# Attention's output: row sums fetched with the products and divided on VectorE

## The reference

```python
w = jax.nn.softmax(scores, axis=-1)
attn = jnp.einsum('bhqk,bkhd->bqhd', w, v).reshape(Bb, Tt, D_MODEL)
return attn @ W_o
...
x = x + ga * _L0_attn_ref(h, ...)
```

## Time and profile before

| | us |
|---|---|
| median of 3 runs | 2197.97 |
| the three runs | 2193.12, 2197.97, 2199.91 |
| the profiled execution | 2178.26 |
| its span in the profile | 2176.7 |

### The profile page before, as it was taken

One profiled execution on the slowest core, in us unless ns is written; L12 is line 12 of the kernel. 1 busy time (PEld: TensorE's weight loads), 2 busy tenths in 40 slices (PEclk: granted clock), 3 DMA queues, 4 the chain that ended last, 5 costly groups with the idle time before them and its releaser, 6 DMA issues. The chain is left out here.

```text
span 2176.7 us, 34681 instructions
## 1 busy us (share of the span) xinstructions
PE 1704.2 (78%) x12628; PEld 841.7 (39%) x12628; DVE 1213.1 (56%) x3101; ACT 859.0 (39%) x1137; POOL 288.6 (13%) x356
## 2 busy tenths in 40 slices
PE   4775268999999999899999366304888887999888
PEld 3332012333333333333333142202444454998566
DVE  3576587877886978687870035301545545101466
ACT  0232034565665666566667204202555513000143
POOL 1000384000000000000000030273222100000011
PEclk8898589999999999999999686656999968999989
DMA  5233942130303030303010130026666200773011
GB/s 174 101 119 136 177 136 71 39 61 26 74 24 65 25 74 26 75 25 74 14 37 26 60 130 0 27 107 152 154 158 153 78 5 6 261 234 121 1 39 48
DMA packets 88965, 180.41 MB, mean 83 GB/s; under 512 B 12529, under 2 KB 61330, under 8 KB 83538
## 3 DMA queue, kind: packets, MB, share of 16 engines
q1 hardware_dynamic: 69072, 109.73, 20.0%
q0 software_dynamic: 18656, 66.31, 9.0%
q10 hardware_dynamic: 1090, 2.36, 0.3%
HBM read 119.38 MB, written 57.85 MB: 81 GB/s over the span
## 5 line engine op out<-in xcount | busy, mean ns | idle before, releaser
L858 ACT ACTIVATE at_pr<-ps 128x1024 f32<-128x1024 f32 (+3 forms) x640 | 548.8, 894 | 358.5 <-PE ps L798 230.3
L892 DVE TENSOR_REDUCE at_mx<-ps 128x1 f32<-128x512 f32 x768 | 488.8, 685 | 168.1 <-PE ps L748 158.5
L795 PE MATMUL ps<-at_sq,at_sk 64*128 64x512 f16 (+3 forms) x2560 | 344.1, 347 | 21.6 <-DMA at_sq<-at_mr 17.8
L748 PE MATMUL ps<-at_sk,at_sq 64*128 64x512 f16 (+3 forms) x1280 | 235.9, 365 | 112.6 <-DMA at_vl<-d_va 41.2
L774 PE MATMUL ps<-at_pr,at_vl 128*32 128x512 f32 (+3 forms) x2560 | 300.6, 541 | 0.1
L889 DVE CUSTOM_DVE_ANT_0 at_seen<-ps,later 128x384 bf16<-128x384 f32 (+3 forms) x512 | 230.0, 488 | 5.4 <-issue 3.8
L798 PE MATMUL ps<-bq,bk 64*128 64x512 f16 (+3 forms) x1280 | 223.9, 346 | 0.0
L748 PEld LDWEIGHTS ps<-at_sk,at_sq 64*128 64x128 f16 x1280 | 61.9, 93 | 409.0 <-DVE at_mx L892 219.1
L795 PEld LDWEIGHTS ps<-at_sq,at_sk 64*128 64x128 f16 x2560 | 112.1, 95 | 126.8 <-ACT at_pr L858 35.7
L1698 PE MATMUL ps<-mi_vn,mi_tz 128*128 x1024 | 144.0, 303 | 2.3 <-DMA mi_tz<-d_z 2.3
L1698 PEld LDWEIGHTS ps<-mi_vn,mi_tz 128*128 128x128 f32 x1024 | 141.4, 191 | 5.1 <-issue 2.7
(11 more groups left out here) (239 smaller groups left out, 2086.8 us busy)
## 6 DMA issues: line engine op xcount, KB each, us to landing
mi_tz<-d_z SPq DMA_DIRECT2D x32, 1024.0 KB, 5.1
ex_w<-d_w POOLq DMA_DIRECT2D x23, 768.0 KB, 6.9
d_rows<-at_nil POOLq DMA_DIRECT2D x32, 379.5 KB, 2.9
ex_xr<-d_rows SPq DMA_DIRECT2D x23, 512.0 KB, 8.2
d_va<-pj_va SPq DMA_DIRECT2D x8, 1024.0 KB, 3.9
at_vl<-d_va SPq DMA_DIRECT2D x8, 1024.0 KB, 12.8
d_o<-at_oc POOLq DMA_DIRECT2D x32, 256.0 KB, 2.3
at_pw<-in_w POOLq DMA_DIRECT2D x24, 256.0 KB, 3.2
```

The costliest lines, as they stand in the source:

```text
L748: ins = pe.matmul(ps[:, MAXB + (slot + r) % RING, 0:hi_ - lo], sq[half[r], b, i, 0, qb * P:(qb + 1) * P], sk[half[r], b, i, 0, lo:hi_], st ...
L795: pe.matmul(ps[:, 2 * f + r, off:CH], sk[half[r], b, f, part, k], sq[half[r], b, f, part, q], start=part == 0, stop=False)
L858: act.activation(pr[:, n % 2, f, :, off:CH], ps[:, 2 * f:2 * f + 2, off:CH], ACT.Exp, scale=INV_SCALE).then_inc(exp_done[f], 1)
L892: ins = dve.tensor_reduce(dst, src, AX.X, ALU.max)
```

## The change

The table of reciprocals in DRAM goes, and with it the loads of `sums`, their two reciprocals, the stores and the loads of `rb`. The chunk loop has three buffers in place of two. For each chunk SP loads the products as before, and ACT's DMA queue loads `total`, rows 16 to 31 of each head, which are 16 equal rows of sums: the same shape as the products. VectorE takes the reciprocal of all of `total` in place (128x1024), and multiplies products and reciprocals into `on`, in place of POOL. It does this for chunk n+1 before it adds the two halves of chunk n to x. TensorE's part is unchanged.

```diff
--- before.py
+++ after.py
@@ -950,50 +950,34 @@
 
         ps = g.ps
         N = NB * NCH
-        sums = sb("sums", [P, NB, T // 8])
-        inv = sb("inv", [P, NB, T // 8])
-        ou = sb("ou", [P, 2, KT, CH])
-        rb = sb("rb", [P, 2, KT, CH])
+        BUF = 3
+        ou = sb("ou", [P, BUF, KT, CH])
+        total = sb("total", [P, BUF, KT, CH])
         on = sb("on", [P, 2, KT, CH])
-        sums_ld = [sem(f"sums_ld{b}") for b in range(NB)]
+        o_ld = [sem(f"o_ld{x}") for x in range(BUF)]
+        t_ld = [sem(f"t_ld{x}") for x in range(BUF)]
         inv_ready = sem("inv_ready")
-        inv_st = [sem(f"inv_st{b}") for b in range(NB)]
-        o_ld = [sem(f"o_ld{x}") for x in range(2)]
         on_ready, w_ready, x_done = sem("on_ready"), sem("w_ready"), sem("x_done")
         d_heads = g.d_o.rearrange("g (h r) n -> (g h) r n", r=32)
         block = c.enter_context(nc.Block())
 
         @block.sync
         def _(sp):
-            for b in range(NB):
-                for h in range(NH):
-                    sp.dma_start(sums[8 * h:8 * h + 8, b, :],
-                                 d_heads[h, HD, b * T:(b + 1) * T].rearrange("(c n) -> c n", c=8))\
-                      .then_inc(sums_ld[b], 16)
-            for b in range(NB):
-                sp.wait_ge(inv_ready, b + 1)
-                sp.dma_start(g.d_r[b].rearrange("h (c n) -> (h c) n", c=8), inv[:, b, :]).then_inc(inv_st[b], 16)
             for n in range(N):
-                b, cols = n // NCH, slice((n % NCH) * CH, (n % NCH + 1) * CH)
-                if n >= 2:
-                    sp.wait_ge(on_ready, n - 1)
+                if n >= BUF:
+                    sp.wait_ge(on_ready, n - BUF + 1)
                 for k in range(KT):
-                    sp.dma_start(ou[:, n % 2, k, :], d_heads[8 * k:8 * k + 8, 0:HD, n * CH:(n + 1) * CH])\
-                      .then_inc(o_ld[n % 2], 16)
-                if n % NCH == 0:
-                    sp.wait_ge(inv_st[b], 16)
+                    sp.dma_start(ou[:, n % BUF, k, :], d_heads[8 * k:8 * k + 8, 0:HD, n * CH:(n + 1) * CH])\
+                      .then_inc(o_ld[n % BUF], 16)
+
+        @block.scalar
+        def _(act):
+            for n in range(N):
+                if n >= BUF:
+                    act.wait_ge(on_ready, n - BUF + 1)
                 for k in range(KT):
-                    sp.dma_start(rb[:, n % 2, k, :],
-                                 g.d_r[b, 8 * k:8 * k + 8, cols].unsqueeze(1).to_broadcast([8, HD, CH]))\
-                      .then_inc(o_ld[n % 2], 16)
-
-        @block.gpsimd
-        def _(pool):
-            for n in range(N):
-                pool.wait_ge(o_ld[n % 2], 16 * 2 * KT * (n // 2 + 1))
-                if n >= 2:
-                    pool.wait_ge(w_ready, 2 * (n - 1))
-                pool.tensor_tensor(on[:, n % 2], ou[:, n % 2], rb[:, n % 2], ALU.mult).then_inc(on_ready, 1)
+                    act.dma_start(total[:, n % BUF, k, :], d_heads[8 * k:8 * k + 8, HD:32, n * CH:(n + 1) * CH])\
+                       .then_inc(t_ld[n % BUF], 16)
 
         @block.tensor
         def _(pe):
@@ -1013,14 +997,24 @@
 
         @block.vector
         def _(dve):
-            for b in range(NB):
-                dve.wait_ge(sums_ld[b], 16 * NH)
-                dve.reciprocal(inv[:, b, :], sums[:, b, :]).then_inc(inv_ready, 1)
-            for m in range(2 * N):
-                dve.wait_ge(w_ready, m + 1)
-                xs = g.x[:, 2 * m:2 * m + 2, :]
-                dve.tensor_tensor(xs, xs, ps[:, m % 8, :].rearrange("p (t c) -> p t c", t=2), ALU.add)\
-                   .then_inc(x_done, 1)
+            def divide(n):
+                dve.wait_ge(t_ld[n % BUF], 16 * KT * (n // BUF + 1))
+                dve.reciprocal(total[:, n % BUF], total[:, n % BUF]).then_inc(inv_ready, 1)
+                dve.wait_ge(o_ld[n % BUF], 16 * KT * (n // BUF + 1))
+                if n >= 2:
+                    dve.wait_ge(w_ready, 2 * (n - 1))
+                dve.wait_ge(inv_ready, n + 1)
+                dve.tensor_tensor(on[:, n % 2], ou[:, n % BUF], total[:, n % BUF], ALU.mult).then_inc(on_ready, 1)
+
+            divide(0)
+            for n in range(N):
+                if n + 1 < N:
+                    divide(n + 1)
+                for m in (2 * n, 2 * n + 1):
+                    dve.wait_ge(w_ready, m + 1)
+                    xs = g.x[:, 2 * m:2 * m + 2, :]
+                    dve.tensor_tensor(xs, xs, ps[:, m % 8, :].rearrange("p (t c) -> p t c", t=2), ALU.add)\
+                       .then_inc(x_done, 1)
 
 
 def phase_route(nc, g):
@@ -1986,7 +1980,6 @@
         g.d_krh = dram("d_krh", [DR, NB * T], F16)
         g.d_va = dram("d_va", [P, NB * NT, NH * 32], F32)
         g.d_o = dram("d_o", [NG, P, NB * T], F32)
-        g.d_r = dram("d_r", [NB, NH, T], F32)
         g.d_w = dram("d_w", [E, P, 3 * 2 * KT * C], F16)
         g.d_rows = dram("d_rows", [NCK * CH, ROW], I32)
         g.d_ws = dram("d_ws", [2, CH], I32)
```

## The result

The changed kernel takes 2206.41 us (median of 17 runs, 2199.16 to 2216.93) against 2194.68 us (17 runs, 2185.05 to 2202.96) for the kernel before. The ratio is 1.0056, with a 95% interval of 1.0040 to 1.0072: slower by 11.7 us, or 9 to 16 us by the interval. The forecast was 13 us slower, 2211 in a range of 2203 to 2220.

A forecast was written before the change was run, and what follows sets the result against it. Loads set the old steps; VectorE would take over the pace. Start 1234.3, eight divisions 62.6, six add pairs 8.3 and tail 6.6 end at 1311.8 against 1298.05: 13 us more after overlap, 2211, range 2203 to 2220.

The forecast's parts named there:

- The bound before: Phase of 72.75 us before: head through DRAM 26.6, seven steps paced by loads at 5.36, tail 4.5; VectorE mostly idle.
- First chunk after 9 us: Head: first chunk lands 9 us after loads start at 1225.30, VectorE starts at 1234.3; bounds 7.3 and 12.0 us.
- One reciprocal 6.56 us: VectorE's 128x1024 reciprocal takes 6.56 us, from 6.25 ns per element on four lengths; bounds 1.75 and 7.01.
- cheap-reciprocal rival: Price per instruction: VectorE's reciprocal of 1024 takes 1.75 us, transfers keep the pace, 19 us less, 2179; chance 0.04.
- Product 1.23 us: VectorE's 128x1024 f32 product takes 1.23 us, priced from one with f16 output; POOL's 2.34 is the other bound.
- Division 7.83 us, cadence 9.2: VectorE per chunk: reciprocal plus product 7.83 us; with two adds of 0.69, 9.2 us against 5.36 of transfers.
- Tail 6.6 us: After the last division, matmuls and two adds take 6.6 us; 4.5 with TensorE warm, 8.5 all cold.
- Loads hidden from chunk 1 on: With three buffers a load has about 18 us and needs 8 to 12, so VectorE sets the pace.
- much slower rival: Chunk loads from two queues stay at 82 GB/s, 12.8 us per chunk; 46 us more, 2244; chance 0.03.
- The sum: Phase ends at 1311.8 against 1298.05, 13.7 us more; 13 after overlap of VectorE instructions, giving 2211 us.
- likeliest case: Whole kernel: +8.7 us (low ends) to +18.6 (first chunk 12.0, tail 8.5), 2206.7 to 2216.6; forecast chance 0.76.

The follow-up runs named there:

- the shortened reciprocal: Changed kernel with the reciprocal cut to 128x256 in place of 128x1024; phase 52.6 us, ratio 0.9917 to the kernel before.
- the run with 16 engines: Changed kernel with a tile's rows reordered (row, then head) so loads use 16 DMA engines; phase 85.3 us, ratio 1.0037 to the kernel before.
- the three runs with steps of 9.0 us and the product on VectorE: Changed kernel, the same with all loads on one queue, and the same with 16 DMA engines; phases 84.8, 85.6 and 85.3 us.

## Why the prediction was right

- **The bound before.** Idle VectorE, a head through DRAM and steps set by transfers were read rightly: the head shrank when its issues were removed, and the steps when the loads ran on more engines. With three buffers and two queues but 8 engines they stayed at 5.2 to 5.4 us (the shortened reciprocal), so the two buffers were not what held them there.
- **First chunk after 9 us.** Measured 8.66, and 8.22 with one queue. It is above the 7.3 us of pure transfer and start; that later chunks in flight share the rate with the first is the likely reason (1.37 MB had come when VectorE started, and 1.66 in the run with 16 engines). No run loaded the first chunk alone.
- **One reciprocal 6.56 us.** Measured 6.546, mean of eight. The line through four lengths held four times further out; the cheap-reciprocal rival is dead by this and by the 3.35 us for 512 columns.
- **Product 1.23 us.** Measured 1.225, the same as with an f16 output.
- **Division 7.83 us, cadence 9.2.** Measured 7.81 (1246.67 - 1238.86) and 9.02. The two adds cost 1.21 us for each step and not 1.38, since neighbouring records overlap. From the first reciprocal to the last product's end it was 69.9 us against 70.9 predicted.
- **Tail 6.6 us.** Measured 1314.96 - 1308.77 = 6.2, between warm (4.5) and cold (8.5). TensorE's 16 matmuls took 3.72 us at best and up to 6.43 in this phase, at a granted clock of 0.72 on average up to 1300. In the three runs with steps of 9.0 us and the product on VectorE the tail was 6.2, 7.5 and 7.2 us.
- **Loads hidden from chunk 1 on.** No wait for them in the changed kernel, so the much slower rival is out.
- **The sum.** 12.0 us in the phase against 13.7, or 13 after overlap. The 1.7 us are 0.3 in front, 1.0 between the first reciprocal and the last product, and 0.4 in the tail, each well inside its bounds. The medians say 11.7 us, so nothing speaks for a gain in the phase behind. The absolute 2211 was 4.6 us high, 3.3 of them because the median of the kernel before was 2197.97 in the three runs I had and is 2194.68 in 17. The 2206.41 lies inside the range, just under the 2206.7 at which the likeliest case began.

The prediction's cheap-reciprocal rival also priced the rest of the change: 19 us less than before if the reciprocal cost no more than one of 256 columns. The shortened reciprocal made that measurable, and it was 20 us. So the mechanism was right on both sides of the balance, and not only in the difference. What the prediction did not ask is how far the rest can go: with the table kept, the same buffers and order take 26 us off the kernel before, together with one load for the sums and 16 engines; the last two alone take 16.6 (23 and 12 us by the ratios).

## What to carry to other kernels

Data repeated for convenience of layout costs again in every instruction that works on it: fetching each sum as 16 equal rows cost no extra bytes here, but gave the reciprocal, at 6.25 ns for each column against 1.2 for a product, sixteen times the elements. Before work is moved to an idle engine, add up what it would do for one step and compare that with the step's present bound, 9.0 against the steady step's 5.36 us here. And the DMA busy share is worth a look: a share that stays at one half under full load may mean that half of the engines get nothing, and the order of a load's dimensions can change that.

## What the hardware showed that I had not expected

Twice as many DMA engines did not give twice the rate for these rows of 2 KB: 238 to 319 GB/s on 16 engines against 202 to 204 on 8. With three chunks in flight the first landed hardly sooner, after 8.2 in place of 8.7 us; with two it landed after 7.7 in place of 12.0, and after 7.5 in place of 10.3 with one load of sums a batch. With two buffers and 16 engines, refills fell into pairs, 3 and 7 us apart.
